# The layer-1 attention product of a two-layer graph network, computed graph by graph on two quadrants of the array

## The reference

```
h    = feat_in @ W                      # 12 heads, 64 columns each
attn = softmax(where(adj, leaky(src + dst^T), -999))
feat_out = elu(attn @ h + b)            # attn is 64 x 64 for each graph and head
gate = sigmoid(feat_in @ H_w.T + H_b)
out  = gate * feat_out + (1 - gate) * feat_in
```

## Time and profile before

| | us |
|---|---|
| median of 3 runs | 2539.49 |
| lowest, highest | 2539.03, 2539.64 |
| the profiled execution: its own time | 2537.7 |
| the profiled execution: span of the trace | 2535.8 |
| PE busy | 2471.5 |
| DVE busy | 2008.2 |
| ACT busy | 912.4 |
| POOL busy | 804.9 |

### The profile page before, as it was taken

How to read it: one execution, slowest core, us unless ns; L and a number is a source line. 1 busy time by engine, 2 the same in 40 slices (tenths; PEclk the granted TensorE clock), 3 DMA queues, 4 the chain that set the end, 5 groups by cost and what they waited for, 6 DMA issues and landing times.

```text
span 2535.8 us, 54256 instructions
## 1 busy us (share of the span) xinstructions
PE 2471.5 (97%) x22592; PEld 1757.2 (69%) x22592; DVE 2008.2 (79%) x2768; ACT 912.4 (36%) x1118; POOL 804.9 (32%) x564
## 2 busy tenths in 40 slices
PE   6999999999999999999999999999999999999994
PEld 5666677776777776777766777766777766777762
DVE  8778777778777778777788787788787788787778
ACT  5433333333333343333333333343333343332332
POOL 1133332333332333322333323333322333323334
PEclk9999999999999999999999999999999999999997
DMA  9243343443343443343443443433443433433432
GB/s 302 42 88 70 81 100 75 81 84 77 81 99 75 81 81 76 85 94 69 92 78 76 88 90 72 93 74 76 92 86 76 87 76 78 94 82 74 81 61 53
DMA packets 552303, 216.98 MB, mean 86 GB/s; under 512 B 517840, under 2 KB 527056, under 8 KB 552272
## 3 DMA queue, kind: packets, MB, share of 16 engines
q1 hardware_dynamic: 552272, 216.53, 40.8%
HBM read 67.02 MB, written 25.17 MB: 36 GB/s over the span
## 4 chain that ended last, share of the span: by engine, by line
PE 94%; DVE 4%; ACT 1%; POOL 1%; DMA 0%; issue 0%; SPq 0%; DVEq 0%
PE pair_prj L574 57%; PE pair_prj L588 29%; PE pair_att L604 3%; PE pair_att L679 2%; PE pair_att L692 1%; PE pair_att L728 1%; DVE w_lo L873 1%; DMA arena<-in_L_gnn_Wq 0%; PE pair_prj L614 0%; PE pair_prj L715 0%; SPq L476 0%; DVE w_top L833 0%; POOL arena L1671 0%; DVE w_hi L962 0%; DVE p_place L1141 0%
## 5 line engine op out<-in xcount | busy, mean ns | idle before, releaser
L574 PE MATMUL pair_prj<-w_hi,arena 128*128 128x512 f16 (+1 forms) x6144 | 1447.5, 327 | 7.8 <-DVE arena L1090 6.9
L574 PE MATMUL pair_prj<-w_lo,arena 128*128 128x512 f16 (+1 forms) x3072 | 1002.5, 326 | 0.0
L574 PEld LDWEIGHTS pair_prj<-w_hi,arena 128*128 128x128 f16 x6144 | 601.6, 98 | 414.3 <-issue 9.1
L588 PE MATMUL pair_prj<-arena,w_hi 128*128 128x256 f16 x4608 | 761.5, 273 | 3.7 <-DVE w_lo L880 3.5
L588 PE MATMUL pair_prj<-arena,w_lo 128*128 128x256 f16 x2304 | 628.9, 273 | 0.0
L588 PEld LDWEIGHTS pair_prj<-arena,w_hi 128*128 128x128 f16 x4608 | 447.2, 98 | 55.4 <-issue 3.6
L574 PEld LDWEIGHTS pair_prj<-w_lo,arena 128*128 128x128 f16 x3072 | 301.1, 98 | 195.3 <-issue 1.7
L1649 POOL TENSOR_TENSOR rstd<-var_eps,minus_half 128x2 f32<-128x2 f32 x63 | 63.0, 999 | 697.8 <-DVE var_eps L898 691.0
L588 PEld LDWEIGHTS pair_prj<-arena,w_lo 128*128 128x128 f16 x2304 | 225.7, 98 | 26.5
L1666 POOL TENSOR_TENSOR arena<-arena,b_row 128x768 f32<-128x768 f32 x60 | 108.6, 1810 | 331.0 <-DVE arena L955 331.0
L1397 ACT ACTIVATE h_hi<-arena,shift,rstd 128x768 f16<-128x768 f32 x124 | 120.6, 1019 | 216.7 <-DVE shift L903 216.7
(11 more groups left out here) (180 smaller groups left out, 2852.7 us busy)
## 6 DMA issues: line engine op xcount, KB each, us to landing
arena<-in_x SPq DMA_DIRECT2D x64, 768.0 KB, 4.3
out<-arena SPq DMA_DIRECT2D x64, 384.0 KB, 2.3
arena<-arena SPq DMA_TRANSPOSE x380, 3.4
arena<-in_L_gnn_Wq SPq DMA_DIRECT2D x2, 1152.0 KB, 8.5
arena<-in_L_gnn_Wk SPq DMA_DIRECT2D x2, 1152.0 KB, 11.8
w_hi<-in_L_gnn_Wv SPq DMA_DIRECT2D x2, 1152.0 KB, 13.4
w_lo<-in_L_gnn_Wf SPq DMA_DIRECT2D x2, 1152.0 KB, 14.4
arena<-in_L_gnn_W SPq DMA_DIRECT2D x2, 1152.0 KB, 13.7
```

The source lines that it names most:

```text
L574: mm = nc.tensor.matmul(pair[:, lo:hi], lhs(a, k), weight(m, k, b)[:, lo:hi], start=(k == 0 and n == 0), stop=(k == KT - 1 and n == 2))
L588: mm = nc.tensor.matmul(pair[:, c * 256:(c + 1) * 256], weight(m, k, a)[:, o:o + P], (ht0_hi, ht0_lo)[b][:, k, :], start=(k == 0 and n == ...
```

## The change

In `attend1` each matmul becomes two, one for each graph b of the tile: rows 64b to 64b + 63 of the stationary and of the moving operand, columns 64b to 64b + 63 of the stationary operand, and output partitions 64b to 64b + 63. The zeros off the diagonal are no longer read. The two write to the same columns c of `pair_att[t]`, on different partitions. The three accumulating parts of one head alternate between the two graphs. `o_psum` is incremented by the last of the 72.

In `attend`, the waits go through `after_held` with a new semaphore `attend_held`. In the loop each is then a wait with an increment of its own; in the unrolled steps it is a plain wait as before.

```diff
+        attend_held = sem("attend_held")
...
                     for n, (pt, hv) in enumerate(parts):
-                        mm = nc.tensor.matmul(pair_att[t][:, c], pt[:, a, :], hv[:, t, c], start=(n == 0), stop=(n == 2))
+                        for b in range(2):
+                            r = slice(b * N, (b + 1) * N)
+                            mm = nc.tensor.matmul(pair_att[t][r, c], pt[r, a, r], hv[r, t, c], start=(n == 0),
+                                                  stop=(n == 2))
                 mm.then_inc(o_psum, 1)
...
                 def attend(t):
                     if t == 0:
-                        pe.wait_ge(h_ready, 2 * p + 2)
-                    pe.wait_ge(pt1_hi_landed[t], GRAPHS * (p + 1))
-                    pe.wait_ge(pt1_lo_landed[t], GRAPHS * (p + 1))
+                        after_held(pe, attend_held, h_ready, 2 * p + 2)
+                    after_held(pe, attend_held, pt1_hi_landed[t], GRAPHS * (p + 1))
+                    after_held(pe, attend_held, pt1_lo_landed[t], GRAPHS * (p + 1))
                     attend1(t, p)
```

## The result

| | us |
|---|---|
| before, median of 4 runs beside it | 2539.56 (2539.03 to 2539.91) |
| after, median of 4 runs | 2556.89 (2555.28 to 2559.06) |
| ratio of after to before | 1.0072, 95% interval 1.006 to 1.0085 |
| profiled execution after: own time, span | 2556.96, 2555.2 |

The change makes the kernel 17.3 us slower (0.7%). The forecast was 2553.5 us, plus 14 us; the time is inside the range 2549 to 2566 and the sign is right, but one term was too small.

What follows compares the result with a forecast made beforehand. PE, busy without a gap through the loop, was taken to bound the kernel. Shape changes of 13.5 us in the loop plus 0.6 us in the last groups, with doubled steps and waits free, gave 2553.5 us; range 2549 to 2566.

Steps and rivals of the forecast that it cites:

- The bound: Loop over groups: PE runs matmul behind matmul without waits, so time added there adds to the 76.45 us period.
- Part 2: Around each attention product: entering and leaving the smaller array shape costs 0.225 us, 13.5 us over 60 products.
- Part 1: Attention product: 72 small matmuls run as 36 pairs of 29.2 ns, 1.05 us as before; cost 0, at most 3 us.
- Part 3: Ahead of each attention product: the separate waits hide behind queued matmuls; cost 0, or 6 us if that cover were gone.
- Part 4: Last two groups: four more attention products change shape, 0.6 us together (0 to 1.6).
- Sum: Whole kernel: the added costs total +14.1 us, giving 2553.5 us, +0.55%.
- A: Attention product: the two quadrants don't run side by side, 2.10 us in place of 1.05; 2621 us, chance 9%.
- B: Ahead of each product: the wait's increment on PE's queue is a barrier, about 0.27 us each; 2570 us, chance 8%.
- C: Product entry and exit: diagonal quadrants pay under 0.085 us for both together, so not slower; 2540 us, chance 4%.

Runs made afterwards that it cites:

- experiment 4: Changed kernel with both tiles' attention products one behind the other, at the second's place, in the loop steps alone: 2669.75 us, ratio 1.0521 to before.
- experiment 1: Four kernels: changed kernel with column halves 2556.82 us, half the moving columns 2555.20, different banks 2556.45; kernel before with 112-column stationary operands 2588.47.
- experiment 3: Kernel before with the new waits alone, the product still 36 full matmuls: 2538.55 us against 2538.19, ratio 1.0002.
- experiment 1's third: Changed kernel with the second graph's heads rotated by 8 of 12, so quadrants write different banks in 8 of 12 head steps: 2556.45 us.
- experiment 2: Changed kernel with all 36 matmuls of the first graph ahead of the second graph's 36, instead of alternating: 2620.73 us.
- experiment 5: Kernel before with the small logit product L715 widened from 36 to 72 stationary columns, extra result rows unused: 2531.45 us against 2538.19, ratio 0.9972.

## Why the prediction was right, and where it was off

- **The bound.** That PE had no slack anywhere in the loop, so that every added 0.1 us counts twice a group, held to 0.01 us in each row of the chain.
- **Part 2, the change of shape.** Forecast 0.225 us in and out, with 0.014 of it for the first load. Shown by the start times: entry 0.093 us over the normal spacing, the first pair 0.020 longer than the later ones, exit 0.096, the next full matmul's spacing 0.010, in all 0.22; experiment 4 takes one change away and gets 0.21 us back. The price is the same for quadrants and column halves, and for the row halves of the context 0.21 us. One sign was loosely put: I had expected 0.2 us again behind the last small matmul, and it is 0.125 us, where two small matmuls in a row stand 0.03 apart.
- **Part 1, the doubled steps: the term that was mis-sized.** I took 29.2 ns a pair, "the doubled steps cost nothing". The pairs take 31.7, plus 36 x 2.5 ns = 0.09 us a product or 5.6 us in 62. The mechanism was in the text (the load of 64 columns against the matmul beside it, "the cover is thin"), but I put the load at 28 ns and allowed it 2.5 ns of its own, from a pair of 58 ns of the scores. If their f32 load counts 128 columns, at the 0.42 ns that experiment 1 shows it takes 53 ns and not the 56 I used, and a pair of 58 ns leaves it 5 ns of its own and not 2.5. I had used 131 columns, read off durations rounded to 1 ns, as if they were exact. My ceiling of 3 us for this term was therefore too low.
- **Part 3, the waits.** Nothing, as forecast (experiment 3).
- **Part 4.** 0.6 us forecast; not resolved. From the 61st product to the end are 69.05 us before and 69.29 after, but 69.25 also in experiment 3, whose product is the old one.
- **Sum.** Forecast 13.5 + 0.6. In the loop steps 18.6 were measured: 13.1 for the change of shape and 5.5 for the loads. Spans of the traces 19.4, medians 17.3.
- **The pages.** The Trainium skill, "TensorE: Matmul & The Clock Gate", section on LDWEIGHTS, gives a load as its columns / 1.2 in ns; by that an estimate is 53 ns for 64 columns and 93 for 112. The runs show 31.7 and 51.7, so the measured values decide; right in direction was that a load of 64 columns ends later than its matmul. The Trainium skill, "TensorEngine Tiling (Array Packing)", section PSUM Pressure, says that different row tiles cannot access one PSUM bank at the same time. Here the two row tiles write different partitions of one bank, and writing to different banks in 8 of 12 head steps changed nothing: 2304.73 us from the first product to the 61st in the changed kernel, 2304.72 in experiment 1's third.
- **Rivals.** A: the quadrants do run side by side (experiment 2). B: experiment 3. C: the entry is 0.20 us and not 0.11.

That the medians are 17.3 us apart and the traces 19.4 lies within the scatter of start and end, which differ from run to run where the loop does not. In seven traces (before, after, the first three kernels of experiment 1, experiments 3 and 5) the first product starts between 180.1 and 182.3 us, and from the 61st to the end are 67.8 to 69.3 us. The kernel before measured 2539.56 us beside the changed one and 2538.19 in 18 later executions, which would make it 18.7. What start and end wait for in one run and not in another stays open, as does the floor named in experiment 1.

## What to carry to other kernels

A product that uses half or a quarter of the array is not free next to full matmuls: here each block of another shape cost about 0.21 us between entry and exit. A stationary operand of other than 128 columns needs, by an estimate from the 0.42 ns a column of experiment 1, about 6 moving columns more than it has stationary ones to hide its load. Two quadrants side by side did only what one full matmul did before, so nothing was gained to set against that price. Give small products 72 stationary columns or more if their neighbours are full: in experiment 5 an operand widened with columns whose result is not read was cheaper than the change of shape. Where PE never waits, look for such blocks first, but leave each where it stands in the order: in experiment 4, moving one 6 us later cost some 18 times what it saved.

## What the runs showed of the hardware

- A matmul with a load of 64 columns follows the last one of its quadrant after 31.7 ns even when only 32 columns are streamed. Two quadrants do this side by side: 72 matmuls take 1.14 us when they alternate and 2.17 us when each quadrant has its 36 in a row.
- 72 stationary columns use the full shape (no gap at entry), as do 108 and 112; 36 and 64 do not, nor do 64 rows (the context). Where between 64 and 72 the limit lies was not tried.
- A wait with an increment on PE's queue is not a barrier: with 145 of them the 60 products of the loop steps took 2286.13 us from the first to the 61st, as without.
